# First attention of a two-layer network: all heads' sums packed in 128 rows, added onto the normalised image, one projection matmul per half image

## The reference

```
x = x + L0_conv(layernorm_over_channels(x))

def L0_conv(xf):                      # xf: [8, 128, 1024]
    normed = groupnorm(xf, 32 groups of 4 channels) * gn_w + gn_b
    q, k, v = split(qkv_w @ normed + qkv_b)        # 8 heads of 16 channels
    weight  = softmax((q * s)^T (k * s), over keys)   # per head, 1024 x 1024
    a = weight @ v                    # put together again: [8, 128, 1024]
    return proj_w @ (xf + a) + proj_b
```

## Time and profile before

| | us |
|---|---|
| median of 3 runs | 2218.71 |
| lowest and highest | 2218.01, 2219.45 |
| the profiled execution | 2221.09 |
| its span, first to last instruction | 2219.2 |
| first attention, first to last group of line 676 | 229.1 to 1007.6 |

### The profile page before, as it was taken

One profiled execution on the slowest core, in us unless ns is written; L12 is line 12 of the kernel. 1 busy time (PEld: TensorE's weight loads), 2 busy tenths in 40 slices (PEclk: granted clock), 3 DMA queues, 4 the chain that ended last, 5 costly groups with the idle time before them and its releaser, 6 DMA issues. The chain is left out here.

```text
span 2219.2 us, 41136 instructions
## 1 busy us (share of the span) xinstructions
PE 1904.9 (86%) x13306; PEld 1065.4 (48%) x13307; DVE 1433.9 (65%) x3154; ACT 1101.3 (50%) x1682; POOL 757.1 (34%) x883
## 2 busy tenths in 40 slices
PE   5668999999999999996699996986669991899993
PEld 2331223333332333323487783654446661799992
DVE  4769898989898998933166665742246663344444
ACT  4550676676767676682144443431125551444443
POOL 0232003142524434254255551000002667355551
PEclk9975999999999999997799998999989985899995
DMA  3860543323232341012333334122101332233326
GB/s 130 178 238 26 72 53 52 54 41 60 40 60 39 60 58 41 12 54 84 96 101 99 96 102 143 57 95 60 33 29 48 116 91 70 77 95 89 88 72 233
DMA packets 134927, 180.01 MB, mean 81 GB/s; under 512 B 44608, under 2 KB 87872, under 8 KB 132480
## 3 DMA queue, kind: packets, MB, share of 16 engines
q1 hardware_dynamic: 116352, 138.25, 26.1%
q0 software_dynamic: 18432, 39.88, 5.4%
HBM read 99.04 MB, written 69.01 MB: 76 GB/s over the span
## 5 line engine op out<-in xcount | busy, mean ns | idle before, releaser
L815 DVE TENSOR_REDUCE mx<-bank 128x1 f32<-128x512 f32 x1024 | 650.0, 696 | 67.6 <-PE bank L590 62.2
L757 ACT ACTIVATE P<-bank 128x1024 f32<-128x1024 f32 x512 | 499.8, 1020 | 291.5 <-PE bank L576 290.3
L1353 POOL DMA_INDIRECT results<-yo,places x284 | 274.2, 966 | 284.0 <-DVE yo L1343 237.9
L590 PE MATMUL bank<-ks,qs 96*128 96x512 bf16 x1024 | 359.3, 402 | 6.7 <-DVE mx L815 6.4
L576 PE MATMUL bank<-qs,ks 99*128 99x512 bf16 x1024 | 295.8, 381 | 2.4 <-ACT P L757 1.6
L1269 PE MATMUL bank<-xt,up 128*128 128x256 f32 x1136 | 277.1, 388 | 3.8 <-DVE xt L1320 1.4
L676 PE MATMUL bank<-P,vt 128*32 128x512 f32 x2048 | 273.6, 606 | 0.7 <-ACT P L757 0.7
L2353 POOL DMA_INDIRECT dispatched<-planes,places x128 | 124.1, 969 | 416.8 <-DVE stats L2197 353.4
L590 PEld LDWEIGHTS bank<-ks,qs 96*128 96x128 bf16 x1024 | 84.2, 98 | 319.7 <-DVE mx L815 251.8
L1269 PEld LDWEIGHTS bank<-xt,up 128*128 128x128 f32 x1136 | 208.0, 193 | 31.8 <-issue 4.4
L1300 ACT ACTIVATE hidden<-bank,rec 128x256 f32<-128x256 f32 x284 | 125.4, 473 | 146.3 <-PE bank L1269 146.3
(11 more groups left out here) (298 smaller groups left out, 2574.1 us busy)
## 6 DMA issues: line engine op xcount, KB each, us to landing
xr<-dispatched SPq DMA_DIRECT2D x142, 130.0 KB
qk_parts<-parts SPq DMA_DIRECT2D x16, 768.0 KB, 5.1
qs<-qk_parts SPq DMA_DIRECT2D x84, 128.0 KB
ks<-qk_parts SPq DMA_DIRECT2D x84, 128.0 KB
v_turned<-vt SPq DMA_DIRECT2D x8, 1024.0 KB, 5.6
vt<-v_turned SPq DMA_DIRECT2D x8, 1024.0 KB
bands<-results SPq DMA_DIRECT2D x32, 256.0 KB, 3.8
y<-results SPq DMA_DIRECT2D x32, 256.0 KB
```

What stands on the lines that cost most here:

```text
L590: pe.matmul(bank[:, slot, :], qs[par][0:KB, h, c * C:(c + 1) * C], ks[par][0:KB, h, half * HALF:(half + 1) * HALF], start=True, stop=True) ...
L757: act.activation(P[:, x % SLOTS, :], bank[:, 2 * pair:2 * pair + 2, :] .rearrange("p a t -> p (a t)"), ACT.Exp).then_inc(probs_ready, 1)
L815: dve.tensor_reduce(mx[:, k // 2, k % 2:k % 2 + 1], bank[:, slot, :], AX.X, ALU.max).then_inc(unit_freed, 1)
L1353: pool.indirect_dma_start(yd_dram, bass.IndirectOffsetOnAxis(places[:, p, q:q + 1], 0), yo[:, p, q, :], None).then_inc(sent[p], 16)
```

## The change

The sums of all eight heads now share 128 rows. For heads 0 to 3 the 16 sum rows of a block of 32 are the first, for heads 4 to 7 the last; the ones columns take the other 16. The reciprocal is taken with a bias column `no_head` that is -1e30 in the rows that hold no sum, so that the reciprocal is zero there. POOL multiplies `o` by `den` in place and then adds `o` onto the half of XF. The channels of XF stand in the order that this gives: the host permutes the centring matrix (`centre_rows`), the group matrix, the weights of q, k, v, of the group normalisation and of the projection. One matmul of `wproj` times XF replaces the three, PARTS["p"] becomes 1, and ORDER is written anew; `wproj_heads` is gone.

```diff
-                        pe.matmul(bank[:, n, :], w["centre"], X[:, bass.ds(cb * T + n * HALF, HALF)],
+                        pe.matmul(bank[:, n, :], w["centre_rows"], X[:, bass.ds(cb * T + n * HALF, HALF)],
...
-ORDER = ("mmmsSmmw", "mmsmSmw", "mmsmSmw", "mmsmSmw", "mmmsSmmw", "mmsmpmpmmSpmw", "mmsmpmpmmSpmw", "mmsmSmw",
-         "mmmstSw", "mmsmtSw", "sSmw", "mmsmlmSmw", "rmsmlmmSmw", "mmsSmw", "mmsmSw", "mmsmSmw",
-         "mmsSmw", "mmsmSw", "msmSmw", "mmsmSw", "mmsmSmw", "mmsmSmw", "mmsSmw", "mmsmSw",
-         "mmmskSmw", "mmmsSmmw", "msmSmw", "mmsmSmmw", "mmsmSmw", "mmrsmSmmw", "mmsmSmw", "mmmsSmmw")
+ORDER = ("mmsmSmw", "mmmsSmmw", "msmSmw", "mmsmSmmw", "mmsmSmw", "mmmspmSmw", "mmmspmSmw", "mmsmSmmw",
+         "mmsmtSw", "mmsmtSw", "msSmw", "mmmslmSmw", "mmslmmrSmw", "mmsSmmw", "mmsmSmw", "mmsmSw",
+         "mmsmSmw", "mmsSmw", "mmsmSmw", "mmsSmw", "mmsmSmw", "mmsmSw", "mmsmSmw", "mmsSmw",
+         "mmmskSmw", "mmmsSmmw", "mmsmSmw", "mmsmSmmw", "mmsmSmw", "mmrsmSmw", "mmsmmSmw", "mmsmSmw")
-PARTS = {"m": 1, "r": 1, "p": 3, "t": 1, "l": 2, "k": 1}
+PARTS = {"m": 1, "r": 1, "p": 1, "t": 1, "l": 2, "k": 1}
...
+            def project(b, n, slot):
+                pe.wait_ge(a_ready, b * 4 + 3 + n)
+                pe.matmul(bank[:, slot, :], w["wproj"], XF[:, bass.ds(b * T + n * HALF, HALF)],
+                          start=True, stop=True).then_inc(unit_filled, 1)
...
-                act.activation(den[:], den[:], ACT.Exp, scale=-1.0).then_inc(rden_ready, 1)
+                act.activation(den[:], den[:], ACT.Exp, scale=-1.0, bias=w["no_head"][:, q // 2:q // 2 + 1]).then_inc(rden_ready, 1)
...
-                dve.stream_shuffle(den[:], o[:], [CH + i % CH for i in range(32)]).then_inc(den_ready, 1)
+                dve.stream_shuffle(den[:], o[:], [(CH if q < 2 else 0) + i % CH for i in range(32)]).then_inc(den_ready, 1)
...
-                if used is not None:
-                    pool.wait_ge(unit_filled, used)
-                g, n = q // 2, q % 2
-                pool.tensor_tensor(a[:, g, n * HALF:(n + 1) * HALF], o[:], den[:], ALU.mult).then_inc(a_ready, 1)
+                pool.tensor_tensor(o[:], o[:], den[:], ALU.mult).then_inc(divided, 1)
+                pool.wait_ge(divided, b * 4 + q + 1)
+                if q >= 2:
+                    pool.wait_ge(a_ready, b * 4 + q - 1)
+                pool.tensor_tensor(cols, cols, o[:], ALU.add).then_inc(a_ready, 1)
...
-                divide(b, 0, plan.number["p", before, 1] if prev else None)
+                divide(b, 0)
...
-FIRST_ONLY = ("group", "wqk", "wv", "bqk", "bv")
+FIRST_ONLY = ("centre_rows", "group", "wqk", "wv", "bqk", "bv")
...
-    wv[:, :, :CH] = qkv[2 * C:].T.reshape(C, HEADS, CH)
+    wv[:, :HEADS // 2, :CH] = qkv[2 * C:].T.reshape(C, HEADS, CH)[:, :HEADS // 2]
+    wv[:, HEADS // 2:, CH:] = qkv[2 * C:].T.reshape(C, HEADS, CH)[:, HEADS // 2:]
...
+    rows = np.arange(C).reshape(2, HEADS // 2, CH).transpose(1, 0, 2).reshape(-1)
+    no_head = np.zeros((HEADS // 2, 2, CH, 2), f4)
+    no_head[:, 1, :, 0] = no_head[:, 0, :, 1] = -1e30
```

More of the change, by code:

```diff
@@ L385, in image @@
             steps.append(pieces)
-        assert count["m"] == MAXIMA and count["p"] == 6 and count["r"] == 2
+        assert count["m"] == MAXIMA and count["p"] == 2 and count["r"] == 2
         return steps
@@ L411, in attend_and_route_first @@
         sem("o_copied"), sem("den_ready"), sem("den_logged"), sem("rden_ready"), sem("a_ready"))
+    divided = sem("divided")
     held, split_held, X_added = sem("held"), sem("split_held"), sem("X_added")
@@ L694, in body @@
                         elif u.kind == "p":
-                            project(u.image, u.at, u.part, u.slot)
+                            project(u.image, u.at, u.slot)
                         elif u.kind == "t":
@@ L710, in last @@
                 for n in range(2):
-                    for part in range(3):
-                        project(B - 1, n, part, 5 + n)
+                    project(B - 1, n, 5 + n)
                 for n in range(2):
@@ L1028, in split_rows, with divide @@
                 split_in_three(pool, nmT[:], nm_rest[:], nm_parts[:], rows_split, b * 2 + g, split_held)
-            def divide(b, q, used=None):
+            def divide(b, q):
+                n = q % 2
+                cols = XF[:, b * T + n * HALF:b * T + (n + 1) * HALF]
                 pool.wait_ge(rden_ready, b * 4 + q + 1)
-                if used is not None:
-                    pool.wait_ge(unit_filled, used)
-                g, n = q // 2, q % 2
-                pool.tensor_tensor(a[:, g, n * HALF:(n + 1) * HALF], o[:], den[:], ALU.mult).then_inc(a_ready, 1)
+                pool.tensor_tensor(o[:], o[:], den[:], ALU.mult).then_inc(divided, 1)
[3 more added lines that the diff above has]
+                pool.tensor_tensor(cols, cols, o[:], ALU.add).then_inc(a_ready, 1)
             def normalize(b):
@@ L2452, in small_tensors @@
         ident=eye, centre=eye - f4(1 / C), mean=np.full((C, C), 1 / C), before_f=np.triu(np.ones((C, C)), 1),
-        group=np.kron(np.eye(C // 4), np.full((4, 4), 0.25)), eps=np.tile([1e-6, 1e-5, 1e-10, 1e-15], (C, 1)),
-        wqk=qkv[:2 * C].T, wv=wv.reshape(C, -1), bqk=qkv_b[:2 * C].reshape(2, C).T, bv=bv.reshape(C, -1),
-        gn=np.stack([I["L0_conv_gn_w"], I["L0_conv_gn_b"]], 1), wproj=proj.T,
-        wproj_heads=proj_heads.reshape(2, C, C).transpose(1, 0, 2).reshape(C, -1), bproj=I["L0_conv_proj_b"].reshape(C, 1),
+        centre_rows=(eye - f4(1 / C))[:, rows],
+        group=np.kron(np.eye(C // 4), np.full((4, 4), 0.25))[rows][:, rows], eps=np.tile([1e-6, 1e-5, 1e-10, 1e-15], (C, 1)),
+        wqk=qkv[:2 * C].T[rows], wv=wv.reshape(C, -1)[rows], bqk=qkv_b[:2 * C].reshape(2, C).T, bv=bv.reshape(C, -1),
+        gn=np.stack([I["L0_conv_gn_w"], I["L0_conv_gn_b"]], 1)[rows], wproj=proj.T[rows],
+        no_head=no_head.reshape(C, 2), bproj=I["L0_conv_proj_b"].reshape(C, 1),
         moe0_router=I["L0_ffn_router_w"], moe0_router_bias=np.tile(I["L0_ffn_router_b"], (C, G)),
```

5 lines of the change are left out of this document (2 added, 3 removed).

## The result

The changed kernel takes 2207.85 us, the median of 5 runs (2201.55 to 2209.87), beside 2219.45 for the kernel before (2218.01 to 2221.28): ratio 0.9941, interval 0.9924 to 0.9958. It is faster by 11.6 us by the medians, by 13.1 by the means, which the ratio follows; 23.8 were forecast, and 2207.85 lies above the range of 2189.5 to 2202. The profiled execution took 2209.87 (span 2208.0).

What follows compares the result with a forecast made beforehand. PE was taken to set the pace of the first attention; 19.2 (images 1 to 6) + 3.4 (image 7) + 1.2 (image 0) = 23.8 us saved, from the median 2218.71 to 2194.9 us, range 2189.5 to 2202.

Steps and rivals of the forecast that it cites:

- Project pieces on PE: First attention: six project pieces become two per image, 3.6 us less, PE's sum falling from 100.2 to 96.6.
- rival 2: First attention: DVE is the bound, nothing is gained, the image keeps about 100 us, time 2218; chance 0.04.
- rival 3: First attention: POOL's added operations hold DVE, 1.9 us lost per image, kernel slower at 2232; chance 0.04.
- The order: New ORDER in the first attention: 0.4 us of stalls per image where DVE falls behind, so 3.2 saved.
- rival 1: First attention: DVE's lags add up to three times the stalls, saving 2.4 us per image, time 2202; chance 0.26.
- Steps 5 and 6: ORDER's two steps with the projection: DVE 3.99 us against PE 4.00 each, level, nothing lost.
- Step 26: ORDER's step now with 4 maxima matmuls where it had 3: loses about 0.15 us waiting for DVE.
- step 11: ORDER's step whose third maxima matmul needs a slot DVE frees late: 0.2 us of stall.
- image 0: First image, without projection: shorter by 1.2 us, 1.6 gained less 0.4 of stalls.
- image 7: Last image, with maxima only up to step 11: saves 3.4 us.
- The end of the stage: I take 0: First attention's end: POOL's addition +1.37, two project records fewer -1.79, net -0.4; ends -0.4 and +1.3, taken as 0.
- The lower edge leaves 1 us for the clock in later stages: Stages behind 1090 us: a change there would show the prediction wrong; 1 us allowed below the best end.

Runs made afterwards that it cites:

- after_again: The changed kernel, unaltered, measured and profiled once more: 2210.50 us, ratio 0.9960 to the kernel before.
- keep_busy: The changed kernel with nine extra matmuls on PE while it waits for POOL in the last image: 2199.18 us, ratio 0.9909.
- pad_36: The changed kernel with 36 empty instructions at the start of TensorE's program, inside its wait for the image: 2206.36 us, ratio 0.9938.
- old_order: The changed kernel with the ORDER of before, keeping one project piece where that had three: 2213.45 us, one run.
- three_projections: The changed kernel with POOL's additions, the ORDER of before and each projection matmul made three times: 2224.84 us, one run.
- late_114: The changed kernel with 114 empty TensorE instructions behind the first attention, in waits for the experts' weights: 2204.56 us, ratio 0.9935.
- same_layout: The changed kernel with 254 unused columns of zeros in the resident weights, so tiles keep the addresses of before: 2207.83 us, ratio 0.9942.
- before_late_142: The kernel before with 142 empty TensorE instructions behind the first attention, in waits for the experts' weights: 2225.12 us, ratio 1.0019.
- divide_early: The changed kernel with POOL's last division and addition moved ahead of eleven of its sixteen sends in the last image: 2193.03 us, ratio 0.9883.
- early_late_114: The changed kernel with the last division ahead of eleven sends and 114 empty TensorE instructions behind the first attention: 2190.05 us, ratio 0.9872.

## Why the prediction was wrong, step by step

**Project pieces on PE: right.** With them and the old order back in, the image is at 100.17 again; DVE as the bound (rival 2) and POOL's additions holding DVE (rival 3) are out: a reduce still takes 0.64 (five in 3.18), and an image with the additions and the old pieces takes what it took.

**The order: right in kind, 0.4 us of stalls mis-sized.** An image loses 97.27 - 96.6 = 0.67; rival 1 wanted 1.2. Steps 5 and 6, "level; nothing lost", take 4.10 instead of 4.00, at DVE's pace; that is 0.2 of the 0.3 missing. Step 26 lost 0.17 as forecast (0.15), step 27 nothing. Steps 11 and 12 take 4.13 + 4.17, where the same pieces took 4.04 + 3.97 before: 0.29 for the 0.2 that was forecast in step 11. Step 30 (5 m) takes 3.15 instead of 3.10. With image 0 (-0.89, forecast -1.2) and image 7 (-2.95, forecast -3.4) the stage's body gives 21.3 of 23.8. That alone would have been 2197, in the range.

**"The end of the stage: I take 0": this step failed.** Its arithmetic held as far as it went: the point where the transposes start lies 20.6 us behind the last group, 21.0 before, a net of -0.4 as worked out. But PE now has its work done sooner and POOL's pair is longer, so its wait grew from 5.78 to 9.23, in which the granted clock stands at 0.50, the 1.2 GHz level, as in the windows above, and it is still there from 1008.0 to 1014.5, with PE full. I priced the clock for the project's records alone (1.7 at most); the logits and the folds behind them paid too. The rank matmul (L653) starts 31.7 behind the last group, 30.1 before; each later fold waits for weights whose load waits for an earlier fold, so what is lost adds up, and the stage ends at 86.9 against 82.7: +4.2, where the prediction's ends for this term were -0.4 and +1.3. In the seven profiles that keep after's order and its wait of 9.2 to 9.5 us the end took 82.9 to 90.6, five of them 86.9 or 87.0; the two with other orders took 85.5 and 85.8 (waits of 6.51 and 3.10); before 82.5 to 82.7, in five of five. In six of the seven the clock was at 0.50 for over 11 us behind the wait's end; the seventh, `after_again`, with some 4 us of it, is the one of 82.9. `keep_busy` against `pad_36`, whose intervals touch, shows that work in the wait takes the loss away: 6.4 us by the ratios. Why `old_order` and `three_projections` lose some 3 us, too, with the clock back sooner behind the wait and low again at later folds, stays open.

**"The lower edge leaves 1 us for the clock in later stages": the other failure.** I took the stages behind 1090 us as unchanged and named a change there as what would prove me wrong; it did. Taking instructions from TensorE's program moved the edges of its instruction blocks in every later stage. In the profiles that is 6.0 us by medians in the convolution and 8.5 in all that lies behind the attention. In whole times it is less: means of -3.5 us for `late_114` against the 16 runs of after, `after_again` and `same_layout`, +4.2 by the ratio of `before_late_142`. That the edges cost time is shown by the latter, with nothing else changed; its interval gives 1 to 7 us. `late_114` and after have intervals that overlap, so the size is not better known.

By the medians 12.2 us are missing (23.8 less 11.6), by the means 10.7. The steps above name 2.5 + 4.2 + some 4 = 10.7; as the last two are known to a few microseconds only, that they fill the gap so well is in part luck. Open stays why `keep_busy` gained 7.2 us more than `pad_36` at the same edge, of which its stage's end explains 3.5. Scatter of the convolution at one edge (138.7 to 144.5) is part of it; what makes it I didn't find.

Of the versions run, `divide_early` at 2193.03 and `early_late_114` at 2190.05 beat both kernels; they differ by no more than their intervals.

## What to carry to other kernels

Before calling the end of a stage "0", look at what the engine does while it waits and at the granted clock behind the wait: work taken from TensorE can make its next wait longer, and everything serial behind it may run at half the clock, so bring the awaited operation forward (here past eleven sends: 14 us) rather than only shortening TensorE's part. Where a stage is made of thousands of tiny matmuls, look for "issue" gaps at a constant count: there an edit upstream that adds or removes TensorE instructions can change the stage by microseconds, for better or worse. Compare a stage over several profiles of both kernels before you explain it.

## What the runs showed of the hardware that was not expected

- In the convolution TensorE stood 0.6 to 1.9 us at 19 to 26 of the 30 edges, one at every 128th pair of load and matmul, that is one per 16 KB of its instructions; beside 2.7 us of work for those 128.
- An instruction that only raises a semaphore took 0.153 us of TensorE's time, from the starts of the runs with 114 and 256 of them.
- Behind its wait of 9.23 us PE worked from 1002.83 to 1014.5 at the lower clock in the profile after. In `after_again`, behind 9.53 us, the fold (L616) took its full-speed 1.88 already 6 us after the wait's end, as PE's timeline shows:

```profile
1005.05 2.08 PE L597 MATMUL bank<-XF,weights 128*128 128x512 f32 x2 [9.53 <-POOL XF L1032]
...
1008.88 2.03 PE L647 MATMUL bank<-router,X 128*128 128x8 f32 x16
...
1011.02 1.88 PE L616 MATMUL bank<-P,vt 128*128 128x512 f32 x4
```

The same program, the same wait: how long the clock stays low differs from run to run, and with it the stage's end (82.9 there).
